# Cross-attention and mixture of experts on one core: another lead-in, tiles in smaller block groups, the output weight turned later, four output buffers

## Chip, core and metric

One core of one Trainium2 chip runs the whole program. The metric is the device time of one execution in microseconds. The inputs are float32.

## What is computed

```python
# x: (2, 2048, 512)   ctx: (2, 128, 512)   mask: (2, 1, 1, 128)
def attention(query, ctx, mask, W_out):            # 16 heads of 32
    energy = einsum('nqhd,nkhd->nhqk', q, k)       # q: layernorm(x), k = v = ctx
    energy = where(mask == 0, -1e20, energy)
    attn = softmax(energy / sqrt(512), axis=-1)
    return einsum('nhqk,nkhd->nqhd', attn, v).reshape(N, Q, 512) @ W_out.T

def ffn(x, proj_w, anchors, temp, w1, w2):         # 6 experts, hidden 256, top 2
    q = tanh(einsum('btd,ed->bte', x, proj_w) / 0.3)
    logits = -(6.0 - einsum('btd,ed->bte', q, anchors)) * 0.5 / clip(temp, 0.1)
    topk_logits, topk_idx = top_k(logits, 2)       # weights: their softmax
    h = gelu(einsum('btd,edh->bteh', x, w1))
    return einsum('bteh,ehd,bte->btd', h, w2, expert_weights)

x = x + attention(layernorm(x), ctx, mask, W_out)
x = x + ffn(layernorm(x), ...)
```

## The kernel before

All engines' programs are written out by hand in one fixed order; nothing is scheduled by a tool. Semaphores tie them together (`wait_ge`, `then_inc`). The 4096 rows are 32 row tiles of 128 (in the last part called token tiles, numbered `c`), four of them are a block, and there are eight blocks (`nblk`), the first four (`NB1`) of batch 0.

**Attention part.** It is a software pipeline over steps `s` from -3 to 44. In step `s` each engine does one piece for several row tiles or units at once; a unit is one block and one group of four heads (`unit(v)`), and there are 32. The lags are constants: a row tile is loaded at `L_LOAD = -3`, its statistics are taken on VectorE at `L_STAT = -1` (with four small GpSimd operations that make its scale), it is normalised on ScalarE (`xn`, L976) at `L_XN = 0`, turned by TensorE (L1667) and copied to `qT` (L938) at `L_XT = 1`. At `L_TOK = 5` TensorE forms a unit's scores by token (L1539) in four PSUM banks (4 to 7), one for each head, only to get their maxima, which VectorE takes (`nmax`, L1103) in the head order 3, 2, 0, 1. At `L_MT = 9` the maxima of a block are turned (L1687) into `mT`. At `L_KEY = 10` come the scores by key (L1560, L1563) in banks 0 to 3, and ScalarE's exponentials (`prob`, L930). At `L_PV = 11` come the row sums (L1697, bank 7) and the products with the values (L1722, bank 6); ScalarE makes the reciprocal of the sums from a logarithm and an exponential (`rden`, L956, L958), and VectorE makes `newton` (L1370) in the same step and `raw` (L1339) one step later. Both have to be done before TensorE may write the next unit's scores by token, because banks 6 and 7 are among the four. From `L_MID = 17` on each step also projects one row tile with the output weight (L1586 to L1588, three products of high and low parts), adds the residual (L1210), and makes the router's logits, choices and places.

**Setup.** Before step -3 the masked keys are turned and filled; the filled keys (`kfT`) are used by the scores by token, the selector rows (`selT`) by the scores by key. The output weight `woraw` is turned in four pieces (L1509), in steps 2 to 5 (`WT0 = 2`), into banks 2 and 3; ScalarE copies a piece to `woH` (L860), VectorE subtracts it for `woL` (L1093). Its first reader is step 17.

**Tables.** The rows of each expert are scattered to a region of their own in `xs_d` (L739). The expert part works on 69 tiles of 128 such rows. Which rows tile w has and which expert it is, stands in a table that VectorE computes. The first `T1 = 27` tiles are full tiles of the first four blocks; their list is made by `full_tiles()` and `first_list()` in steps 40 and 41. The other 42 come in classes: class c has the tiles that become complete, or begun, with the first NB1 + c blocks. Their list is made in slots 19 to 23 of the expert part. `TILES_OF` tells for a block how many tiles must be done before all its rows are.

**Expert part.** It is a loop of 76 slots; in slot j tile w = j - 2 is turned (L1763), w = j - 3 goes through the first layer (L1777 to L1779), w = j - 4 is turned again (L1787), w = j - 5 goes through the second (L1803 to L1805), and its result is copied to `ysb` (VectorE for w below 26, then ScalarE, L1032) and stored to `y_d` in slot w + 6 (SyncE, L641). `ysb` has two buffers, each used again when its store has landed. From slot 46 on a finished token tile is put together in each slot: two slots before, GpSimd gathers its two expert rows from `y_d` (L809, two indirect transfers); VectorE adds them, weighted, to the residual (`put_together`, L1408, L1410); SyncE stores it two slots later (L601) and loads a residual for 16 tiles later three slots after that (L607). Token tiles 28 to 31 need all 69 tiles and come after the loop. SyncE's queue is in order: xg loads, y stores, output stores and residual loads wait for each other.

## Time and profile before

| | us |
|---|---|
| median of three runs | 640.44 (638.33 to 643.96) |
| the profiled execution's own time | 639.05 |
| its span in the trace | 636.2 |
| TensorE matmuls busy | 557.3 (88%) |
| VectorE busy | 419.2 (66%) |
| ScalarE busy | 343.7 (54%) |
| GpSimd busy | 303.4 (48%) |

Busy time is the sum over a span whose parts have different limits, so a share says little by itself; a stretch and the wait that ends last in it say more. Times in the rows are from the start of the span.

### The profile page before, as it was taken

The page shows a single profiled execution, that of the slowest core. Times are in us where ns is not written, and L with a number is a line of the kernel's source. Part 1 is how long each engine was busy: PE and PEld are TensorE (multiplying, and loading weights), DVE is VectorE, ACT ScalarE, POOL GpSimd, SP SyncE. Part 2 cuts the span into 40 slices and gives each one's busy share as a digit, 9 for nine tenths or more (in the row PEclk, how much of TensorE's full clock was granted, in tenths as well). Part 3 has the DMA queues.
Part 4 walks back from the last instruction along what each step waited for, and adds up shares of the span by engine and source line. Part 5 has one row for each costly group of instructions (what it writes and reads, how often), then busy time and mean ns, then how long its engine had stood idle before and what let it go on. Part 6 is the DMA issues. An engine that isn't in the chain of part 4 may idle for free.

```text
span 636.2 us, 14210 instructions
## 1 busy us (share of the span) xinstructions
PE 557.3 (88%) x4472; PEld 409.1 (64%) x4472; DVE 419.2 (66%) x895; ACT 343.7 (54%) x664; POOL 303.4 (48%) x434
## 2 busy tenths in 40 slices
PE   5668899999999999899787999998999999999950
PEld 3554355565555555545475897887999998987730
DVE  4677777667678776748799555567843356666643
ACT  3648875777767656466556663532355544443420
POOL 5434765655548666485688041331000155555443
PEclk9779999999999999999997999998999999999995
DMA  5321132233213329373558374786567799999986
GB/s 167 101 67 51 52 97 88 83 101 100 100 50 101 134 84 344 104 265 133 171 177 282 103 246 157 242 281 216 191 224 233 220 293 357 401 405 405 365 298 186
DMA packets 60274, 122.07 MB, mean 192 GB/s; under 512 B 7718, under 2 KB 10790, under 8 KB 60204
## 3 DMA queue, kind: packets, MB, share of 16 engines
q1 hardware_dynamic: 49964, 87.61, 40.9%
q0 software_dynamic: 10240, 33.56, 14.8%
q8 instruction: 40, 0.66, 0.4%
q14 instruction: 30, 0.25, 0.1%
HBM read 67.93 MB, written 53.22 MB: 190 GB/s over the span
## 4 chain that ended last, share of the span: by engine, by line
PE 64%; DVE 13%; issue 10%; DMA 4%; ACT 4%; POOL 3%; SPq 0%; POOLq 0%; DVEq 0%; ACTq 0%
PE ps L1777 5%; PE ps L1779 4%; PE ps L1697 4%; PE ps L1778 4%; PE ps L1803 4%; PE ps L1805 4%; PE ps L1804 4%; PE ps L1763 4%; PE ps L1560 4%; PE ps L1539 4%; PE ps L1586 4%; PE ps L1588 3%; PE ps L1587 3%; PE ps L1722 3%; DMA y_d<-ysb 2%
## 5 line engine op out<-in xcount | busy, mean ns | idle before, releaser
L809 POOL DMA_INDIRECT yg<-y_d,y_row x64 | 66.7, 1041 | 129.0 <-DMA y_d<-ysb 74.6
L739 POOL DMA_INDIRECT xs_d<-x,to_row x64 | 66.8, 1043 | 70.0 <-DVE to_row L1185 34.2
L930 ACT ACTIVATE prob<-ps 128x512 f32<-128x512 f32 x128 | 65.9, 600 | 53.0 <-PE ps L1563 52.8
L1103 DVE TENSOR_REDUCE nmax<-ps 128x4 f32<-128x512 f32 x128 | 79.5, 685 | 21.4 <-PE ps L1539 21.4
L1777 PE MATMUL ps<-w1H,xgH 128*128 x276 | 84.0, 305 | 4.9 <-issue 4.4
L1421 DVE TENSOR_TENSOR xgL<-ps,xgH 128x512 fp32r<-128x512 f32 x69 | 47.5, 689 | 53.5 <-ACT xgH L1012 44.0
L1779 PE MATMUL ps<-w1L,xgH 128*128 x276 | 78.1, 283 | 0.0
L1778 PE MATMUL ps<-w1H,xgL 128*128 x276 | 77.9, 282 | 0.0
L1803 PE MATMUL ps<-w2H,hH 128*128 x138 | 60.3, 437 | 1.3 <-DVE ysb L1436 1.2
L769 POOL TENSOR_TENSOR atT<-less,raw 128x512 f32<-128x512 f32 x32 | 40.9, 1279 | 42.6 <-issue 36.8
L1777 PEld LDWEIGHTS ps<-w1H,xgH 128*128 128x128 f32 x276 | 52.8, 191 | 7.9 <-issue 7.6
L1032 ACT ACTIVATE ysb<-ps 128x512 f32<-128x512 f32 x43 | 25.8, 599 | 55.8 <-DMA y_d<-ysb 30.8
L1012 ACT ACTIVATE xgH<-ps 128x512 fp32r<-128x512 f32 x69 | 41.1, 595 | 25.3 <-PE ps L1763 21.7
L1805 PE MATMUL ps<-w2L,hH 128*128 x138 | 54.5, 395 | 0.0
L1586 PE MATMUL ps<-woH,atH 128*128 128x512 f32 x128 | 52.9, 413 | 1.5 <-DVE x L1210 1.2
L1804 PE MATMUL ps<-w2H,hL 128*128 x138 | 54.1, 392 | 0.0
L1778 PEld LDWEIGHTS ps<-w1H,xgL 128*128 128x128 f32 x276 | 53.0, 192 | 0.0
L1019 ACT ACTIVATE gel<-ps 128x256 f32<-128x256 f32 x69 | 26.6, 386 | 48.1 <-PE ps L1779 40.7
L1779 PEld LDWEIGHTS ps<-w1L,xgH 128*128 128x128 f32 x276 | 52.6, 191 | 0.0
L1429 DVE TENSOR_TENSOR hL<-ps,hH 128x256 fp32r<-128x256 f32 x69 | 29.1, 421 | 33.7 <-ACT hH L1025 29.4
L1539 PEld LDWEIGHTS ps<-kfT,qT 32*128 32x128 f32 x1024 | 33.5, 190 | 26.7 <-issue 26.3
L1588 PE MATMUL ps<-woH,atL 128*128 128x512 f32 x128 | 50.0, 391 | 0.0
(214 smaller groups left out, 1296.5 us busy)
## 6 DMA issues: line engine op xcount, KB each, us to landing
xg<-xs_d SPq DMA_DIRECT2D x69, 256.0 KB
y_d<-ysb SPq DMA_DIRECT2D x69, 256.0 KB
xin<-in_x SPq DMA_DIRECT2D x32, 256.0 KB, 2.7
x<-in_x SPq DMA_DIRECT2D x32, 256.0 KB, 3.0
x_d<-x SPq DMA_DIRECT2D x32, 256.0 KB
x2t<-x_d SPq DMA_DIRECT2D x32, 256.0 KB
out_x<-x2t SPq DMA_DIRECT2D x32, 256.0 KB
w1L<-in_L_ffn_w SPq DMA_DIRECT2D x6, 512.0 KB, 8.2
```

What stands on the lines that cost most here:

```text
L739: nc.gpsimd.indirect_dma_start(xs_d, bass.IndirectOffsetOnAxis(ap=to_row[:, n, k, t:t + 1], axis=0), x2[:, n % 4, t, :], None).then_inc(sc ...
L809: nc.gpsimd.indirect_dma_start(yg[:, c % RY, z, :], None, y_d[0:TILES_OF[c // 4] * P, :], bass.IndirectOffsetOnAxis(ap=y_row[:, c, z:z + 1 ...
L930: nc.scalar.activation(prob[v % 2][:, h, :], ps[:, B_SC + h, :], ACT.Exp, scale=scale).then_inc(exp_done, 1)
L1103: nc.vector.tensor_reduce(nmax[:, n % 2, :, g * hpg + h], ps[:, token_bank(h), :].rearrange("p (t k) -> p t k", t=4), axis=AX.X, op=ALU.ma ...
L1586: mm(o, h[:, g, :], woH[:, g, :], start=(g == 0), stop=False)
L1588: last = mm(o, l[:, g, :], woH[:, g, :], start=False, stop=(g == kchunks - 1))
L1777: mm(o, xgH[:, p, c, :], w1h[:, cols], start=(c == 0), stop=False)
L1778: mm(o, xgL[:, p, c, :], w1h[:, cols], start=False, stop=False)
L1779: last = mm(o, xgH[:, p, c, :], w1l[:, cols], start=False, stop=(c == kchunks - 1))
L1803: mm(o, hH[:, p, c, :], w2h[:, cols], start=(c == 0), stop=False)
L1804: mm(o, hL[:, p, c, :], w2h[:, cols], start=False, stop=False)
L1805: last = mm(o, hH[:, p, c, :], w2l[:, cols], start=False, stop=(c == halves - 1))
```

## The change

Four things are joined.

1. Lead-in. Statistics of the first four row tiles, the filled keys and the selectors are interleaved otherwise; the scores by token of units 1 and 3 go to banks 0 to 3 (`token_bank`, up to unit `SOON = 5`) and those of units 0, 2 and 4 to banks 4 to 7; the turned row tile goes to a bank that is free (`turned_bank`). `raw` of units 0 to 5 is formed in the same step as `newton`, before it.
2. Output weight. It is turned in steps 10 to 13 (`WT0 = L_KEY`), through one bank. ScalarE copies each piece twice, to `wot` and to `woH`; GpSimd forms `woL` from these. The router's projection follows in step 14. Small GpSimd constants move from steps 1 to 3 to steps 4 to 6.
3. Block groups. The full tiles of the first four blocks are listed with those of the first three blocks ahead. All tokens of the first three blocks are then complete after 32 tiles instead of 37. The last block is counted in two halves, so that token tiles 28 and 29 need 65 tiles and only 30 and 31 need all 69. Token tiles are put together from slot 41 on, five in six slots (slots 41 to 45, 47 to 51, ..., 68), those of the last two blocks in slots 70 to 75, and only 30 and 31 after the loop.
4. `ysb` has four buffers (`RW = 4`).

```diff
-    TILES_OF = [most_tiles(max(n + 1, NB1)) for n in range(nblk)]
-    CLASSES = nblk - NB1 + 1
+    TILES_OF = [T1 + EXPERTS - 1 if n + 1 < NB1 else most_tiles(n + 1) for n in range(nblk) for t in range(4)]
+    TILES_OF[4 * nblk - 4] = TILES_OF[4 * nblk - 3] = most_tiles(nblk - 0.5)
+    CLASSES = nblk - NB1 + 3
-    RY, RX, RD = 6, 16, 4
+    RY, RX, RD, RW = 6, 16, 4, 4
-        B_CNT, B_SEL, B_WT, B_FILL, B_KT = 2, 2, 2, 4, 6
+        B_CNT, B_SEL, B_WT, B_FILL, B_KT = 2, 2, 1, 4, 6
+        SOON = 5
-        def token_bank(h):
-            return B_MX + h
+        def token_bank(v, h):
+            return (B_MX if v >= SOON or v % 2 == 0 else B_SC) + h
+        def turned_bank(w):
+            v = w + L_XT - L_TOK
+            return B_XT if v <= 0 or v + 1 >= SOON else token_bank(v - 1, TOKEN_ORDER[0])
...
         def put_slot(c):
-            s = TILES_OF[0] + 9 + c
-            return s if s < SLOTS and TILES_OF[c // 4] < tiles else None
+            w = TILES_OF[0] + 9 + c + c // 5
+            if c // 4 >= nblk - 2:
+                w = TILES_OF[c] + 9 + c - TILES_OF.index(TILES_OF[c])
+            return w if w < SLOTS and TILES_OF[c] < tiles else None
-        WT0 = 2
+        WT0 = L_KEY
...
# GpSimd
+                c = s - WT0
+                if 0 <= c < kchunks:
+                    pool.wait_ge(s_woR, c + 1)
+                    pool.wait_ge(s_woH, c + 1)
+                    nc.gpsimd.tensor_tensor(woL[:, c, :], wot[:, c, :], woH[:, c, :], ALU.subtract).then_inc(s_woL, 1)
...
# ScalarE
-                    nc.scalar.activation(woH[:, c, :], ps[:, B_WT + c % 2, :], ACT.Copy).then_inc(s_woH, 1)
+                    nc.scalar.activation(wot[:, c, :], ps[:, B_WT, :], ACT.Copy).then_inc(s_woR, 1)
+                    nc.scalar.activation(woH[:, c, :], ps[:, B_WT, :], ACT.Copy).then_inc(s_woH, 1)
...
+                if 0 < s < 4:
+                    rows_normalised(s - L_XN)
+
                 w = s - L_XT
...
                     nc.scalar.activation(qT[n % 3][:, :, t * P:(t + 1) * P],
-                                         ps[:, B_XT, :].rearrange("p (k t) -> p k t", k=kchunks), ACT.Copy).then_inc(qT_done, 1)
+                                         ps[:, turned_bank(w), :].rearrange("p (k t) -> p k t", k=kchunks), ACT.Copy).then_inc(qT_done, 1)
+                setup(s)
...
+                if not 0 < s < 4:
+                    rows_normalised(s - L_XN)
+                if s == 3:
+                    filled_keys()
+                if s == L_TOK:
+                    selectors()
...
-                        after(act, y_out[p], 16 * n)
-                        nc.scalar.activation(ysb[:, p, :], ps[:, y_bank(w, p), :], ACT.Copy).then_inc(ya_done, 1)
+                        _, r, n = tl(i, k, L_DN, RW)
+                        after(act, y_out[r], 16 * n)
+                        nc.scalar.activation(ysb[:, r, :], ps[:, y_bank(w, p), :], ACT.Copy).then_inc(ya_done, 1)
...
# VectorE
             def attention(s):
-                d = s - L_DIV
...
+                if s >= L_MID + 1:
+                    raw_product(s - L_DIV)
...
+                setup(s)
+                if s <= L_MID - 1:
+                    raw_product(s - L_PV)
...
# TensorE, scores by token and by key
-                pe.wait_ge(qT_done, 4 * n + 4)
+                pe.wait_ge(qT_done, max(4 * n + 4, min(v + L_TOK - L_XT, 4 + SOON - 1)))
+                if v == 1:
+                    pe.wait_ge(s_selT, batches)
-                after(pe, mx_done, hpg * v)
+                after(pe, mx_done, hpg * (v if v >= SOON else v - 1))
...
+                after(pe, s_woH, min(v + L_KEY - WT0, kchunks))
```

On TensorE, from the key fill to the second scores by token, before (`xn` is the normalised row tile, `selk` the selector rows, `kfill` the filled keys):

```order
L1483 MATMUL ps<-kmask,pickb 128x512 x2
L1488 MATMUL ps<-ident,selk 128x128 x8
L1495 MATMUL ps<-ident,kfill 128x128 x8
L1667 MATMUL ps<-ident,xn 128x128 x8
L1509 MATMUL ps<-ident,woraw 128x128 x4
L1667 MATMUL ps<-ident,xn 128x128 x4
L1509 MATMUL ps<-ident,woraw 128x128 x4
L1667 MATMUL ps<-ident,xn 128x128 x4
L1509 MATMUL ps<-ident,woraw 128x128 x4
L1539 MATMUL ps<-kfT,qT_78 128x128 x16
```

and now:

```order
L1553 MATMUL ps<-kmask,pickb 128x512 x2
L1745 MATMUL ps<-ident,xn 128x128 x12
L1566 MATMUL ps<-ident,kfill 128x128 x8
L1745 MATMUL ps<-ident,xn 128x128 x4
L1559 MATMUL ps<-ident,selk 128x128 x8
L1606 MATMUL ps<-kfT,qT_78 128x128 x16
```

The row tiles are turned ahead of the filled keys and the selectors, and the output weight is gone from here.

On VectorE, the end of `first_list()` in step 41, before (`ntil` counts tiles of an expert, `whole` the full ones, `taken` and `some` belong to the two groups of the new list):

```order
L1261 TENSOR_REDUCE lexpert<-prod 128x1
L1262 TENSOR_SCALAR lst<-lexpert 128x1
L1271 TENSOR_SCALAR ntil<-first 128x6
L1272 TENSOR_SCALAR ntil<-ntil 128x6
L1273 TENSOR_TENSOR ntil<-ntil,whole 128x6
L1339 TENSOR_TENSOR raw<-ps,rden 128x512
```

and now:

```order
L1323 TENSOR_REDUCE lexpert<-prod 128x1
L1324 TENSOR_SCALAR lst<-lexpert 128x1
L1335 TENSOR_SCALAR taken<-first 128x12
L1336 TENSOR_SCALAR taken<-taken 128x12
L1337 TENSOR_TENSOR taken<-taken,some 128x12
L1338 TENSOR_TENSOR ntil<-taken 128x6
L1339 TENSOR_TENSOR ntil<-ntil,soon 128x6
L1407 TENSOR_TENSOR raw<-ps,rden 128x512
```

Two operations are added here, two more at the list's beginning, and `full_tiles()` a step earlier has fourteen instead of six.

On VectorE, in the expert slots about the fifth and sixth token tile, before (`x2t` is the residual that becomes the output, `yg` the gathered rows):

```order
L1408 SCALAR_TENSOR_TENSOR x2t<-yg,share,x2t 128x512 [waits yg_in4,x2t_in0]
L1410 SCALAR_TENSOR_TENSOR x2t<-yg,share,x2t 128x512 [waits half_done]
L1421 TENSOR_TENSOR xgL<-ps,xgH 128x512 [waits xh_done]
L1429 TENSOR_TENSOR hL<-ps,hH 128x256 [waits hh_done]
L1408 SCALAR_TENSOR_TENSOR x2t<-yg,share,x2t 128x512 [waits yg_in5,x2t_in1]
```

and now:

```order
L1477 SCALAR_TENSOR_TENSOR x2t<-yg,share,x2t 128x512 [waits yg_in4,x2t_in0]
L1479 SCALAR_TENSOR_TENSOR x2t<-yg,share,x2t 128x512 [waits half_done]
L1490 TENSOR_TENSOR xgL<-ps,xgH 128x512 [waits xh_done]
L1498 TENSOR_TENSOR hL<-ps,hH 128x256 [waits hh_done]
L1490 TENSOR_TENSOR xgL<-ps,xgH 128x512 [waits xh_done]
L1498 TENSOR_TENSOR hL<-ps,hH 128x256 [waits hh_done]
L1477 SCALAR_TENSOR_TENSOR x2t<-yg,share,x2t 128x512 [waits yg_in5,x2t_in1]
```

After five token tiles a slot without one is left.

## Rows read from the trace of the kernel before

**Rows 1.** Timeline, 0 to 30 us: start, us, engine, line, operation, [idle before].
```profile
7.76 3.17 PE L1483 MATMUL ps<-kmask,pickb 128*128 128x512 f32 x4
...
10.14 0.25 POOL L782 TENSOR_SCALAR nmr<-mrs 128x1 f32<-128x1 f32 x1
...
14.21 0.83 ACT L976 ACTIVATE xn<-xin,nmr,rstd 128x512 f32<-128x512 f32 x1
...
24.03 1.17 PE L1539 MATMUL ps<-kfT,qT 32*128 32x128 f32 x32
```

**Rows 2.** Timeline, 29 to 60 us: token scores, first scores by key.
```profile
31.76 1.17 PE L1539 MATMUL ps<-kfT,qT 32*128 32x128 f32 x32 [1.77 <-DVE nmax L1103]
32.13 0.69 DVE L1346 BATCH_NORM_STATS2 st<-xin 128x6 f32<-128x512 f32 x1
...
32.99 2.48 DVE L1103 TENSOR_REDUCE nmax<-ps 128x4 f32<-128x512 f32 x4
...
35.63 1.17 PE L1539 MATMUL ps<-kfT,qT 32*128 32x128 f32 x32 [2.10 <-DVE nmax L1103]
...
42.93 2.09 PE L1560 MATMUL ps<-qT,kT 32*128 32x512 f32 x8 [0.78 <-ACT mT L950]
```

**Rows 3.** Timeline, 55 to 63 us: one round of the ring.
```profile
55.86 1.17 PE L1539 MATMUL ps<-kfT,qT 32*128 32x128 f32 x32 [0.62 <-DVE raw L1339]
...
57.88 1.06 PE L1697 MATMUL ps<-prob,ones 128*32 128x512 f32 x8 [0.27 <-issue]
...
60.91 0.68 DVE L1339 TENSOR_TENSOR raw<-ps,rden 128x512 f32<-128x512 f32 x1
...
61.74 1.17 PE L1539 MATMUL ps<-kfT,qT 32*128 32x128 f32 x32 [0.62 <-DVE raw L1339]
```

**Rows 4.** Timeline of VectorE, 296 to 318 us.
```profile
303.55 0.69 DVE L1210 TENSOR_TENSOR x<-ps,x 128x512 f32<-128x512 f32 x1 [1.28 <-PE ps L1588]
...
310.50 0.17 DVE L1273 TENSOR_TENSOR ntil<-ntil,whole 128x6 f32<-128x6 f32 x1
...
312.06 1.13 DVE L1192 TENSOR_TENSOR wgt<-wsel,winv 128x24 f32<-128x24 f32 x1
```

**Rows 5.** Stretches: busy PE, PEld, DVE, ACT, POOL (count), clock, DMA share, GB/s.
```profile
500.00:550.00 50.00, 48.73 (x337) 43.92 (x336) 28.50 (x47) 23.94 (x55) 25.85 (x24) 1.00 0.92 317
...
550.00:560.00 10.00, 10.00 (x72) 9.13 (x71) 8.02 (x13) 4.25 (x11) 5.84 (x6) 1.00 1.04 405
...
590.00:600.00 10.00, 9.01 (x61) 7.69 (x60) 6.70 (x12) 3.56 (x10) 4.54 (x5) 1.00 1.04 394
```

**Rows 6.** The page: DMA queue, one group of ScalarE, one DMA issue.
```profile
q0 software_dynamic: 10240, 33.56, 14.8%
...
L1032 ACT ACTIVATE ysb<-ps 128x512 f32<-128x512 f32 x43 | 25.8, 599 | 55.8 <-DMA y_d<-ysb 30.8
...
xg<-xs_d SPq DMA_DIRECT2D x69, 256.0 KB
```

**Rows 7.** Timeline of TensorE: turns of xg tiles 55, 56 and 66.
```profile
557.88 0.60 PE L1763 MATMUL ps<-ident,xg 128*128 128x128 f32 x4
...
561.35 0.60 PE L1763 MATMUL ps<-ident,xg 128*128 128x128 f32 x4
...
601.85 0.60 PE L1763 MATMUL ps<-ident,xg 128*128 128x128 f32 x4
```

**Rows 8.** Timeline, 608 us to the end.
```profile
610.19 1.43 POOL L809 DMA_INDIRECT yg<-y_d,y_row  x1 [0.31 <-issue]
...
612.53 0.39 PE L1805 MATMUL ps<-w2L,hH 128*128 x1
...
614.47 0.60 ACT L1032 ACTIVATE ysb<-ps 128x512 f32<-128x512 f32 x1 [2.69 <-DMA y_d<-ysb]
...
617.91 0.95 POOL L809 DMA_INDIRECT yg<-y_d,y_row  x1 [6.30 <-DVE x2t L1410]
...
627.16 0.95 POOL L809 DMA_INDIRECT yg<-y_d,y_row  x1 [0.30 <-issue]
```

More of the change, by code:

```diff
@@ L257, in xattn_moe @@
         lst = sb("lst", [P, 2])
-        zero_row1 = sb("zero_row1", [P, EXPERTS])
-        bound = sb("bound", [P, EXPERTS, CLASSES + 1])
-        moveby = sb("moveby", [P, EXPERTS, CLASSES + 1])
-        change = sb("change", [P, EXPERTS * (CLASSES + 1)])
-        within = sb("within", [P, 2 * 4, EXPERTS * (CLASSES + 1)])
+        zero_row1 = sb("zero_row1", [P, 2, EXPERTS])
+        soon = sb("soon", [P, EXPERTS])
+        some = sb("some", [P, 2, EXPERTS])
+        taken = sb("taken", [P, 2, EXPERTS])
+        nsoon = sb("nsoon", [P, 1])
+        bound = sb("bound", [P, EXPERTS, PLACES])
+        moveby = sb("moveby", [P, EXPERTS, PLACES])
+        change = sb("change", [P, EXPERTS * PLACES])
+        within = sb("within", [P, 2 * 4, EXPERTS * PLACES])
         moved = sb("moved", [P, 2 * 4])
@@ L914, in exponentials, with rows_normalised @@
                     nc.scalar.activation(lexp[:], ldif[:], ACT.Exp).then_inc(lexp_done, 1)
+            def rows_normalised(w):
+                if live(w, ntile):
+                    n, t = w // 4, w % 4
+                    act.wait_ge(rstd_done, 4 * w + 4)
+                    act.wait_ge(x_in[t], 16 * (n + 1))
+                    after(act, xt1_ready, w - 1)
+                    nc.scalar.activation(xn[:, w % 2, :], xin[:, t, :], ACT.Identity, bias=nmr1[:, t, :],
+                                         scale=rstd1[:, t, :]).then_inc(xn_done, 1)
             def attention(s):
@@ L1051, in link, with statistics @@
                 dve.wait_ge(s_set, chain[0])
+            def statistics(w):
+                n, t = w // 4, w % 4
+                dve.wait_ge(x_in[t], 16 * (n + 1))
+                after(dve, mv_done, w - 3)
+                nc.vector.bn_stats(st1[:, t, :], xin[:, t, :]).then_inc(st_done, 1)
+                dve.wait_ge(st_done, w + 1)
+                after(dve, rstd_done, 4 * (w - 3))
+                nc.vector.bn_aggr(mv1[:, t, :], st1[:, t, :]).then_inc(mv_done, 1)
             link(nc.vector.tensor_scalar(m01[:], maski[:], 0.0, None, ALU.not_equal))
@@ L1637, in prefix @@
                                   allones[:].bitcast(F32R), sel[:, t:t + 1, :].bitcast(F32R).to_broadcast([P, 4 - t, EXPERTS]), start=False, stop=(t == 3))
+                    if n == nblk - 1:
+                        for t in range(2):
+                            last = mm(ps[:, b, PL0 + 5 * EXPERTS:PL0 + 6 * EXPERTS], allones[:].bitcast(F32R),
+                                      sel[:, t, :].bitcast(F32R), start=(t == 0), stop=(t == 1))
                     last.then_inc(pl_ready, 1)
```

200 lines of the change are left out of this document (109 added, 91 removed).

## The prediction

> **What bounds the kernel now.** I read the span stretch by stretch, since the limit changes. The reader should see five things.
>
> First, the start. The four row tiles of block 0 must be normalised, turned and copied before any scores can be made. VectorE, ScalarE and TensorE hand each other one tile at a time. The scale of the first tile is there at 10.14 + 0.25 = 10.39 us, TensorE has finished the key fill at 7.76 + 3.17 = 10.93 us, and yet ScalarE writes the first normalised tile only at 14.21 and the first scores by token start at 24.03 [rows 1]. In between stand the two key copies, the two selector copies and the output weight.
>
> Second, from 24 to 43 us each step takes 35.63 - 31.76 = 3.87 us [rows 2]: scores 1.17, then four maxima 2.48 on VectorE, and TensorE waits for these because the four banks are the same ones. The first scores by key come at 42.93.
>
> Third, up to step 17 a ring through three engines sets the pace [rows 3]: scores at 55.86, one maximum, row sums at 57.88, their logarithm and its exponential on ScalarE, newton and then raw (60.91) on VectorE, next scores at 61.74. The period is 5.88 us. From step 18 TensorE is nearly full until about 300 us, then VectorE carries the chain to about 350 us; the first tile table stands in that chain [rows 4].
>
> Fourth, in the expert part TensorE needs 561.35 - 557.88 = 3.47 us for a slot, but the ten slots to 601.85 take 40.50 us [rows 7]: 5.8 us too many. What is late is a buffer. ScalarE stood 30.8 us in waits for stores of y_d before its copies into ysb [rows 6]. The stores are late because the DMA engines are full: 405 GB/s at a share of 1.04, 394 near the end, while the mean of 500 to 550 us was 317 [rows 5].
>
> Fifth, the end. TensorE is done at 612.53 + 0.39 = 612.92 us and the span ends at 636.2. The last copy waited 2.69 us for a buffer, the last store had landed by 617.91, and only then do eight gathers of four token tiles start, the last at 627.16 [rows 8].
>
> **Start, steps -1 to 9.** Statistics of tiles 0 and 1 move ahead of the selector rows, so the scale comes about 0.6 us earlier, at 9.8. TensorE now turns tile 0 right after the key fill, at 10.95. Each round is a normalisation (0.83, [rows 1]), a turn of four transposes (0.60, [rows 7]; up to twice that while TensorE has the lower of its clocks) and a copy (0.60 for this size, [rows 8]), and the normalisation of the next tile stands ahead of the copy: 1.3 to 1.8 us a round. VectorE gives the fourth statistic only after the filled keys. I make three rounds end near 16.2, then the fill transposes, the fourth turn and the selector transposes (eight, four and eight: 2.3 us if all follow at once): first scores at 18.5, 5.5 us earlier. In steps 5 to 9 the scores alternate between banks 4 to 7 and 0 to 3. The step is then VectorE's: 2.48 + 0.87 (from the statistics at 32.13 to the maxima at 32.99, [rows 2]) + 0.1 = 3.45, so 0.4 less for each of three steps. One step is late by about 1 us, because the selector copies now stand on ScalarE before the second scores. The last hand-over (maxima, nmhl, turn, mT) loses a half microsecond of TensorE queue. I put the first scores by key at 36.2 instead of 42.93: **6.7 us earlier**. Bounds: 3 (TensorE slow at the start, one more late load) and 9.
>
> **Output weight, steps 10 to 14.** It leaves a stretch in which ScalarE waits for the others and goes to one in which it stands in the ring. Each of four steps gets four more transposes (0.60), and two ScalarE copies (0.6 each, one of them new) that stand ahead of the logarithm of the ring. The sums end about 0.4 us later, and the logarithm starts 0.5 later. In step 10 there is no sum yet, but the next scores by key wait for woH: 1.1 us. Sum 1.1 + 3 x 0.45 + 0.1 for projT = **2.5 us later**. If all of it hides it is 0; if nothing does, 4 x (0.6 + 1.2) = 7.2. I stay near the lower end: between the maximum and the sums' logarithm the ring leaves ScalarE some two microseconds, and only what the copies need beyond that counts. The subtraction for woL goes from VectorE to GpSimd, which is off the ring except in step 13. Putting raw before newton changes nothing in the ring, as both must be done before the next scores. Net for both parts: **-4.2 us**, from 0 to -9.
>
> **Tile tables.** The first table gets eight more VectorE operations of about 0.2 us (0.17 is a typical one, [rows 4]) at 300 us and four more in the list at 307. The eight run into an idle of 1.28 us that VectorE spends waiting for the projection at 303.55 [rows 4], so 1.65 - 1.28 = 0.4 us shows. The four are in the chain: 0.8. Sum **+1.2**; 0.8 if all eight hide. The later tables gain two classes, one operation and two small matmuls beside expert slots, where VectorE is busy 28.50 of 50 us [rows 5]: at nothing, 0.5 us if not.
> Two operations of the same size took 1.13 us at 312.06 [rows 4] and 0.17 elsewhere, with GpSimd at work beside the long ones. The Trainium skill, SBUF — State Buffer, section "Who interferes with whom", says that a VectorE operation with two SBUF inputs and a GpSimd operation that reads SBUF shut each other out for a whole instruction. By that rule this group could cost about 4 us rather than 1.2.
> From the rows alone the upper bound is 12 x 0.35, a third of the operations being long: 4.3.
>
> **Gathers in 5 of 6 slots, 5 slots earlier, and four y buffers.** A slot loads one xg tile and stores one y tile (0.26 MB each, [rows 6]). A token tile costs 0.26 MB four times: two gathers (33.56 MB in 128 indirect transfers), one residual load, one store. Before, with a token tile in each slot, 0.524 + 1.049 = 1.573 MB in 3.47 us asks 454 GB/s; the rows show 405 [rows 5], so it falls behind. After, with 5 of 6 slots, 1.398 MB ask 403 GB/s, at the capacity and no more, and the five earlier slots use a time when 317 was moved. Four ysb buffers let a store be late by about 10 us. So I take the whole 5.8 us back: **-5.8**. Bounds: 0 if the stores stay late past four buffers, and -7 if slots before tile 56 had lost a little too.
>
> **The end.** The last half block waits for all 69 tiles, the half before it for 65, so four gathers move ahead of the last store. Relative to before: GpSimd ends tile 27's gathers at 610.19 + 1.43 = 611.6, then six steps of 1.3 us (9.25 us for seven gaps at the end, [rows 8]) bring the first gather of tile 31 to about 619.7 and its second to 621.0. The last store follows the matmuls by one copy, 613.7 with no buffer wait. From the end of that copy to the first gather went 617.91 - 615.07 = 2.8, so it is there by 616.5 and does not bind. 621.0 instead of 627.16: **-6.1**. The landing, the combination and the last store, 9.0 us from 627.16 to the end, stay as they are. Bounds: -4 (the store lands late and binds) and -8 (less traffic, quicker landings).
>
> **Sum.** -4.2 + 1.2 - 5.8 - 6.1 = -14.9. The profiled execution was 639.05 us, span 636.2 and 2.85 around it: 639.05 - 14.9 = 624.2. The median of the three runs lies 1.4 above it, so I say **624.5**.
>
> **Rivals.**
> (a) The DMA engines stay full and the stores stay late, so the slots gain nothing; the end still has four gathers less (5.3). -4.2 + 1.2 - 5.3 = -8.3: 631. For it: 403 is no margin, and the window rows are means over 10 us. Against: four buffers.
> (b) The lead-in gives nothing, since the output weight eats it: -10.7: 628.5. For it: ScalarE stands in the ring in those steps. Against: 6.7 before 2.5.
> (c) The transfers carry less than the rows show when gathers, residual loads and y traffic all mix for 28 slots. Those slots took 28 x 3.47 + 5.8 = 103.0 us. Halfway between 405 and 317, at 361 GB/s, they would take 28 x 1.398 / 0.361 = 108.4 us: +5.4 - 8.3 = -2.9, 636. The rows show 405 for 30 us on end [rows 5], which speaks against it.
> The Trainium skill, DMA: Bandwidth & Descriptors, section "Where 436 GB/s comes from", says that between HBM and SBUF a side of about 358 GB/s binds; by that rule (c) holds, at 109.3 us and 637, and the trace disagrees with 405 GB/s.
> (d) Slower: the same mechanism, deeper. SyncE's queue is in order; if a combination waits for its gather, the store of its rows blocks the xg loads behind it, and each slot then lasts as long as its transfers. The time passes the old one by 1% once 28 x 1.398 / c is over 103.0 + 8.3 + 6.4 = 117.7 us, that is below c = 333 GB/s. At the 317 of 500 to 550 us it is 123.5: +20.5 - 8.3 = +12.2, 653. For it: that mean holds at a share of 0.92. Against: the windows after it show 405, so 317 was demand and not capacity.
>
> **Chances.** Forecast 0.62 (its own range 617 to 629), (a) 0.12, (b) 0.12, (c) 0.09, (d) 0.05. The range reaches from 616 to 635. Over 1% (6.4 us, about what a measurement can tell from no change) faster means below 634: forecast, (a) and (b), 0.86. Within 1%: (c) and a part of the rest, 0.09. Slower: 0.05.
>
> **What would show it.** The first scores by token near 18.5 us, the first by key near 36, four steps after them at 6.3 to 6.5 us, and step 18 some 4 us earlier. First list 0.8 us longer. No waits of ScalarE for y_d stores worth naming, xg turns 3.47 us apart through tile 66, DMA near 400 GB/s from the fifth slot of gathers on but stores landed in time. After the last matmul some 17 us instead of 23.3, with four gathers after the last store. Wrong it would be if gathers or stores from slot 41 on hold back the xg loads, or if steps 10 to 13 run over 7 us.

## The result, and the profile after

The changed kernel takes **622.82 us** (median of four runs, 619.53 to 623.75) against 639.73 for the kernel before (median of four, 638.33 to 643.96). The ratio is 0.9717, 95% interval 0.9664 to 0.977. The forecast was 624.5, with a range from 616 to 635. The profiled execution took 619.53 us, span 617.7, against 639.05 and 636.2: 18.5 us less span, where the sum of the prediction had 14.9.

The stretches of the span, each read from TensorE's starts (turns of `xg` are counted from tile 0; by this count the turns at 557.88, 561.35 and 601.85 of [rows 7] are tiles 57, 58 and 68, not 55, 56 and 66):

| | before | after | difference | predicted |
|---|---|---|---|---|
| first scores by token | 24.03 | 17.22 | -6.8 | -5.5 |
| scores by token of step 10 | 45.20 | 36.20 | -9.0 | -6.7 |
| ... of step 18 | 94.33 | 87.56 | -6.8 | -4.2 |
| ... of step 36 | 258.05 | 251.82 | -6.2 | -4.2 |
| turn of tile 2 | 350.86 | 346.05 | -4.8 | -3.0 |
| end of the last matmul | 612.92 | 597.28 | -15.6 | -8.8 |
| end of the span | 636.2 | 617.7 | -18.5 | -14.9 |

The timeline of TensorE and VectorE in the start, of the changed kernel (start, us, engine, line, operation, idle before); it answers to [rows 1, 2]:

```profile
7.79 2.97 PE L1553 MATMUL ps<-kmask,pickb 128*128 128x512 f32 x4
...
10.62 0.66 PE L1745 MATMUL ps<-ident,xn 128*128 128x128 f32 x4
...
17.22 1.17 PE L1606 MATMUL ps<-kfT,qT 32*128 32x128 f32 x32
...
21.38 1.17 PE L1606 MATMUL ps<-kfT,qT 32*128 32x128 f32 x32 [2.41 <-issue]
...
23.83 1.17 PE L1606 MATMUL ps<-kfT,qT 32*128 32x128 f32 x32 [0.69 <-ACT qT L981]
...
25.83 2.45 DVE L1151 TENSOR_REDUCE nmax<-ps 128x4 f32<-128x512 f32 x4
...
26.27 1.17 PE L1606 MATMUL ps<-kfT,qT 32*128 32x128 f32 x32 [0.69 <-ACT qT L981]
...
29.02 2.45 DVE L1151 TENSOR_REDUCE nmax<-ps 128x4 f32<-128x512 f32 x4
...
33.94 2.09 PE L1632 MATMUL ps<-qT,kT 32*128 32x512 f32 x8 [0.78 <-ACT mT L994]
```

TensorE now makes the scores of a unit while VectorE still reads the unit before. So three of its steps are 2.44 us, each with a wait of 0.69 us for ScalarE's copy of the turned row tile, and no longer VectorE's: the maxima start 3.19 us apart (25.83, 29.02). The first step is 4.16 us (17.22 to 21.38): the selector copies end on ScalarE at 21.28, just ahead of the second scores. TensorE waits for VectorE only once, at the end of the steps:

```profile
31.02 0.63 PE L1745 MATMUL ps<-ident,xn 128*128 128x128 f32 x4 [1.12 <-DVE nmax L1151]
```

The ring with the output weight in it, the same timeline, 49 to 54 us; it answers to [rows 3]:

```profile
49.85 1.06 PE L1782 MATMUL ps<-prob,ones 128*32 128x512 f32 x8
...
50.02 0.59 ACT L890 ACTIVATE wot<-ps 128x512 f32<-128x512 f32 x1
50.49 0.60 ACT L891 ACTIVATE woH<-ps 128x512 fp32r<-128x512 f32 x1
...
50.98 0.60 ACT L1000 ACTIVATE rden<-ps 128x512 f32<-128x512 f32 x1
...
52.34 0.69 DVE L1407 TENSOR_TENSOR raw<-ps,rden 128x512 f32<-128x512 f32 x1 [0.64 <-ACT rden L1002]
...
52.95 0.68 DVE L1440 TENSOR_TENSOR newton<-ps,rden 128x512 f32<-128x512 f32 x1
...
53.97 1.17 PE L1606 MATMUL ps<-kfT,qT 32*128 32x128 f32 x32 [0.89 <-DVE newton L1440]
```

The logarithm (L1000) follows the second copy without a gap, and the next scores by token follow the second of the two products. The steps from 12 to 17 last 6.25, 6.59, 6.25, 6.14 and 5.98 us, against 5.88 before (6.26 in the second of them).

Stretches of the expert part of the changed kernel (busy time and count of PE, PEld, DVE, ACT, POOL; then clock, DMA share, GB/s); they answer to [rows 5]:

```profile
500.00:550.00 50.00, 50.00 (x348) 45.25 (x347) 33.42 (x55) 25.33 (x59) 23.84 (x23) 1.00 1.04 392
...
550.00:560.00 10.00, 10.00 (x71) 9.04 (x70) 5.97 (x10) 5.03 (x12) 6.03 (x6) 1.00 1.04 407
...
590.00:600.00 10.00, 7.27 (x39) 5.67 (x37) 5.54 (x9) 3.59 (x8) 7.87 (x7) 1.00 0.92 293
```

The DMA engines are as full as at their fullest before (1.04, 392 and 407 GB/s), and for longer; yet TensorE is busy all the time. Its turns (answering to [rows 7]) are:

```profile
553.02 0.60 PE L1847 MATMUL ps<-ident,xg 128*128 128x128 f32 x4
...
556.48 0.60 PE L1847 MATMUL ps<-ident,xg 128*128 128x128 f32 x4
...
587.49 0.60 PE L1847 MATMUL ps<-ident,xg 128*128 128x128 f32 x4
```

Ten slots, 553.02 to 587.49, take 34.47 us where they took 40.50. In the list of waits ScalarE's copy into `ysb`, 30.8 us for stores before [rows 6], does not wait for a store at all.

The end of the changed kernel, answering to [rows 8]:

```profile
596.88 0.40 PE L1889 MATMUL ps<-w2L,hH 128*128 x1
...
597.31 0.60 ACT L1074 ACTIVATE ysb<-ps 128x512 f32<-128x512 f32 x1 [0.94 <-issue]
...
598.70 0.41 SPq L662 DMA_DIRECT2D y_d<-ysb  x1
...
600.39 0.95 POOL L836 DMA_INDIRECT yg<-y_d,y_row  x1 [0.30 <-issue]
...
604.62 0.99 POOL L836 DMA_INDIRECT yg<-y_d,y_row  x1 [3.28 <-DMA y_d<-ysb]
...
608.93 0.95 POOL L836 DMA_INDIRECT yg<-y_d,y_row  x1 [0.30 <-issue]
```

Four gathers follow the last store instead of eight, but the first of the four waits for that store: 6.7 us from the end of the copy (597.91) to 604.62, where it was 2.8 before, there behind a copy that had itself waited 2.69 us for a store [rows 8]. From the last matmul to the end of the span it is 20.4 us instead of 23.3.

### The profile page after: what moved, and what is told of

The parts are those of the page before. It is cut to its first block, busy times and chain, and to the rows that moved or that the text cites. A ratio compares the mean times of both kernels' runs of the same rounds, so it can differ in the third digit from the quotient of the medians.

```text
span 617.7 us, 14277 instructions
## 1 busy us (share of the span) xinstructions
PE 545.1 (88%) x4474; PEld 402.4 (65%) x4474; DVE 424.3 (69%) x905; ACT 345.5 (56%) x668; POOL 308.8 (50%) x438
## 3 DMA queue, kind: packets, MB, share of 16 engines
q0 software_dynamic: 10240, 33.56, 14.9%
## 4 chain that ended last, share of the span: by engine, by line
PE 64%; DVE 16%; issue 8%; ACT 6%; POOL 2%; DMA 2%; POOLq 0%; SPq 0%; DVEq 0%; ACTq 0%
PE ps L1861 5%; PE ps L1863 5%; PE ps L1862 5%; PE ps L1887 5%; PE ps L1889 5%; PE ps L1888 5%; PE ps L1847 5%; PE ps L1632 4%; PE ps L1658 4%; PE ps L1782 4%; PE ps L1660 3%; PE ps L1659 3%; ACT prob L970 3%; PE ps L1807 3%; PE ps L1606 2%
## 5 line engine op out<-in xcount | busy, mean ns | idle before, releaser
L1863 PE MATMUL ps<-w1L,xgH 128*128 x276 | 76.8, 278 | 0.0
L1659 PE MATMUL ps<-woL,atH 128*128 128x512 f32 x128 | 50.0, 391 | 0.0
```

Of the source, the lines that this page charges most:

```text
L1659: mm(o, h[:, g, :], woL[:, g, :], start=False, stop=False)
L1863: last = mm(o, xgH[:, p, c, :], w1l[:, cols], start=False, stop=(c == kchunks - 1))
```

## The experiments

Each ratio is to the kernel before, measured beside the variant (medians of 638.43 to 639.87), with its 95% interval. The totals of one kernel differ by some microseconds from execution to execution, so the readings rest on two stretches of one profile each: **slots**, from the turn of tile 23 to the end of the last matmul, and **tail**, from there to the end of the span. Eight profiles (changed, and the last seven rows) have the same expert slots, but for the last tiles in two of them. Their slots took 165.3 to 167.8 us, so a difference of up to 2.5 us says little. The tails with four gathers behind the last store lie between 18.6 and 21.2 us.

| kernel | median, us | ratio (interval) | slots | tail |
|---|---|---|---|---|
| before | 639.73 | 1 | 174.5 | 23.3 |
| changed | 622.82 | 0.9717 (0.9664 to 0.977) | 165.3 | 20.4 |
| before, four `ysb` | 636.77 | 0.9963 (0.9934 to 0.9991) | 173.6 | 23.2 |
| changed, two `ysb` | 627.36 | 0.9831 (0.9776 to 0.9887) | 171.0 | 19.0 |
| every slot | 632.62 | 0.9897 (0.9857 to 0.9938) | 173.8 | 19.0 |
| every slot to 19 | 627.23 | 0.9792 (0.9766 to 0.9819) | 170.3 | 18.7 |
| from slot 46 | 629.35 | 0.9821 (0.9772 to 0.9871) | 171.6 | 21.2 |
| last block whole | 625.85 | 0.982 (0.9783 to 0.9856) | 166.0 | 23.7 |
| old banks | 624.98 | 0.9799 (0.9758 to 0.9839) | 165.3 | 19.5 |
| weight not turned | 619.7 | 0.9721 (0.9691 to 0.9751) | 166.4 | 18.6 |
| one copy | 622.26 | 0.9758 (0.9726 to 0.979) | 165.3 | 19.5 |
| newton first | 625.36 | 0.9762 (0.9735 to 0.9789) | 167.8 | 20.7 |
| ScalarE's stores | 625.42 | 0.978 (0.9749 to 0.9812) | 166.4 | 19.8 |
| filled | 621.31 | 0.9702 (0.9661 to 0.9743) | 166.0 | 19.2 |

### Buffers or rate

Four buffers alone, in the kernel before:

```diff
-        ysb = sb("ysb", [P, 2, emb])
+        ysb = sb("ysb", [P, RW, emb])
...
-                        after(act, y_out[p], 16 * n)
+                        after(act, y_out[r], 16 * n)
```

> The kernel before with four ysb buffers and nothing else changed. Theory 'buffers' (what was late was the buffer, and two more of them, 2 x 3.47 = 6.9 us of lateness, hide nearly all of it): no waits of ScalarE on stores of y_d but a few at the very end, last matmul 6 to 8 us earlier than 612.92, 632 to 634 us in all. Rival 'rate' (each slot asks 1.57 MB in 3.47 us, 454 GB/s against 405, a deficit of about 0.4 us in each of 28 slots; the backlog then shows at the xg loads and the gathers instead): last matmul at most 3 us earlier, 637 to 640 us.

Slots 173.6 against 174.5, last matmul 2.1 us earlier, total 0.4% less (636.77 us, just under the rival's 637): the rival "rate" was right. In the profile ScalarE's wait for stores is gone, and these waits (us in total, times, longest) stand in its place:

```profile
POOL yg L809 <- DMA y_d<-ysb: 10.3, 2, 6.0
...
PEld ps L1765 <- DMA xg<-xs_d: 5.1, 6, 1.4
...
PE ps L1765 <- DMA xg<-xs_d: 2.2, 3, 1.0
```

The stretches from 540 to 600 us show 405, 405 and 402 GB/s at a share of 1.04: the same full engines. A buffer more only hands the lateness on, from the stores to the loads.

Two buffers in the changed kernel:

```diff
-    RY, RX, RD, RW = 6, 16, 4, 4
+    RY, RX, RD, RW = 6, 16, 4, 2
```

> The changed kernel with two ysb buffers again. Theory 'buffers': the stores are late by more than one slot at a DMA share of 1.04, so ScalarE waits again and the last matmul moves from 597.28 to 600.5 or later; 626 us or more. Rival 'rate' (five token tiles in six slots keep the transfers within capacity, the buffers are spare): waits on y_d stores under 3 us in sum, last matmul within 1 us of 597.28, 622 to 624 us.

Slots 171.0, 5.7 us more than with four; here "buffers" was right. The waits of this kernel:

```profile
ACT ysb L1074 <- DMA y_d<-ysb: 21.3, 13, 4.7
```

One of them alone was 4.70 us, ahead of the copy at 522.98, and TensorE's two slots around it took 10.97 us instead of 6.9. So with the old slots two more buffers are worth 0.9 us, which is not clear of the scatter, with the new ones 5.7; the slots (with their block groups) are worth 3.5 us with two buffers and 8.3 with four. Neither half explains the gain; each needs the other.

Token tiles in every slot from 41:

```diff
-            w = TILES_OF[0] + 9 + c + c // 5
+            w = TILES_OF[0] + 9 + c
```

> The changed kernel with a token tile in every slot from slot 41 to 64 (no slot left out), four buffers. Theory 'buffers': the 24 slots ask 454 GB/s, fall behind by up to 24 x 0.4 = 10 us, which is more than four buffers hold; a stall of 2 to 4 us late in that stretch, given back by nothing; end as now or 1 us shorter since slots 65 to 69 carry no gathers: 623 to 626 us. Rival 'rate' (the left-out slot is what keeps the pace): 627 us or more. If it costs nothing (within 1 us of 622.8), the left-out slots are worth nothing by themselves.

Slots 173.8: 8.5 us more, the expectation of "rate". But the profile shows a second cause. At 563.20 GpSimd had waited for the store of the last expert tile that token tile 20 needs:

```profile
563.20 0.95 POOL L836 DMA_INDIRECT yg<-y_d,y_row  x1 [7.27 <-DMA y_d<-ysb]
...
570.44 0.75 DVE L1477 SCALAR_TENSOR_TENSOR x2t<-yg,share,x2t 128x512 f32<-128x512 f32 x1 [5.41 <-DMA yg<-y_d,y_row]
...
572.71 0.19 PEld L1861 LDWEIGHTS ps<-w1H,xgH 128*128 128x128 f32 x1 [3.58 <-issue]
```

GpSimd waits for the store, VectorE in its combination for the gather, and behind that stand the subtractions TensorE needs. A second kernel took this away, and left the rate up to tile 19:

```diff
-            w = TILES_OF[0] + 9 + c + c // 5
+            w = TILES_OF[0] + 9 + c + (4 if c >= 20 else 0)
```

> The changed kernel with token tiles 0 to 19 in every slot from 41 to 60 and 20 to 23 where the changed kernel has them (65 to 68). With every slot to tile 23 the run was slower by 9 to 10 us, and in it GpSimd waited 7.27 us for a store of y_d ahead of the gathers of tile 20, since these come only one slot behind the store of the last expert tile that tile 20 needs. Theory 'caught up with its block': that wait alone made the loss; here it is gone and the pace holds: from the turn at slot 25 to the last matmul about 165 to 168 us as in the changed kernel, 622 to 625 us. Rival 'rate': 454 GB/s asked in 20 slots against 405 leaves a backlog of 20 x 0.4 = 8 us that four buffers do not hold: that stretch takes 170 us or more, 628 us or more.

Slots 170.3, the edge of what "rate" asked, and 627.23 us, just short of its 628. So 5.0 of the 8.5 us come with a token tile in each of the first twenty slots, and the other 3.5 with token tiles 20 to 23 in slots 61 to 64. These 3.5 hold the wait for the block, but also four more slots at the full rate, since slots 61 to 64 have no token tile in the second kernel; the two were not separated.

The old slots (one each from 46 to 69) with four buffers and the new groups:

```diff
-            w = TILES_OF[0] + 9 + c + c // 5
+            w = TILES_OF[0] + 14 + c
```

> The changed kernel with the old slots for the first 24 token tiles (one in every slot from slot 46 to 69), four buffers, the last eight as changed. Theory 'buffers': a backlog without time to clear before the end, last matmul 2 to 4 us later than 597.28 and the end longer by 1 us: 625 to 628 us. Rival 'rate': the last matmul 5 us or more later, 628 us or more. If it is within 1 us of 622.8, start and rate of the token tiles are worth nothing once there are four buffers.

Slots 171.6, 6.3 more; 629.35 us, and the last matmul at 608.06 (part of that lateness stems from the start, which ran at a lower clock). That is "rate" again. The loads of `xg` are late by 6.1 us in sum, and with a token tile in every slot from 46 to 75 there is none in which the backlog clears.

### The end

The last block not counted in halves:

```diff
-    TILES_OF[4 * nblk - 4] = TILES_OF[4 * nblk - 3] = most_tiles(nblk - 0.5)
```

> The changed kernel, but token tiles 28 and 29 wait for all 69 tiles again, so that eight gathers follow the last store. Theory 'four gathers less' (they cost 1.3 us each on GpSimd after the landing): the last gather starts 5.3 us later than 608.93, if the last store lands at the same 604.6; 627 to 629 us. Rival 'the last store is late because of them' (the gathers of 28 and 29, issued at 596.2 to 600.4, stand before the last store's packets in full DMA engines): without them the store lands near 600.7, the first of eight gathers starts then, the last at about 609.6, and the whole is within 1.5 us of 622.8.

The tail is 23.7, against 20.4 and, in the other profiles with the changed tail, 18.6 to 21.2: the half block is worth 2.5 to 5 us, 3.3 by the changed kernel's own profile. The first gather came at 602.44, 5.0 us after the end of the last copy (596.82 + 0.60), with no gathers of tiles 28 and 29 ahead. So these explain at most 1.7 of the 6.7 us, and even that is not shown: in the ten other profiles with the changed tail, with those gathers ahead, this time is 4.9 to 7.3 us. The last of the eight gathers started at 611.33, 2.4 later than 608.93, not 5.3 and not 0.7.

Why the store lands later than the 2.8 us of the kernel before can be read from the kernel before with four `ysb`:

```profile
610.86 0.60 ACT L1033 ACTIVATE ysb<-ps 128x512 f32<-128x512 f32 x1 [1.19 <-PE ps L1807]
...
615.53 0.94 POOL L809 DMA_INDIRECT yg<-y_d,y_row  x1 [6.01 <-DMA y_d<-ysb]
```

It has the old tail, but its last copy need not wait for a buffer, and then the gather starts 4.1 us after the copy. Counted from the last matmul it is 4.7 us (610.82 to 615.53), and 5.0 in the kernel before (612.92 to 617.91). The lateness moved from the copy to the store.

The last four stores issued by ScalarE:

```diff
+        OWN = 4
...
+                        if w >= tiles - OWN:
+                            act.wait_ge(ya_done, w + 1 - BY_ACT)
+                            nc.scalar.dma_start(y_d[w * P:(w + 1) * P, :], ysb[:, r, :]).then_inc(y_out[r], 16)
```

> The changed kernel, but the stores of the last four expert tiles are issued by ScalarE itself right behind its copy, and not by SyncE. Theory 'queue': the last store is late (gathers of tiles 30 and 31 start 6.7 us after the end of the last copy, against 2.8 before) because it stands behind output stores and waits in SyncE's order; from a queue of its own the gathers start 4 to 4.5 us after the copy, and the last store of the program comes 2 to 2.5 us earlier: 620.5 us, time from the last matmul to the end about 17.5 us. Rival 'engines full': the store's packets share the sixteen DMA engines with gathers, and another queue changes nothing: gathers start 6 to 7 us after the copy, 622.8 us, tail 19 to 20.5.

The gathers began at 609.24, 4.9 us after the copy's end. That is near what "queue" expects, but four profiles in which SyncE issues the stores have 4.9 to 5.1 us as well (two `ysb`, weight not turned, every slot to 19, newton first), so the queue's part is not shown. And the copy itself came late, and nothing was gained (tail 19.8):

```profile
603.75 0.60 ACT L1075 ACTIVATE ysb<-ps 128x512 f32<-128x512 f32 x1 [2.27 <-remote]
```

The profile does not name what it waited for. In the program the copy waits for two things, its matmuls and the store that used its buffer four tiles earlier, and the matmuls had ended at 601.63. So by elimination, which no row shows, it waited for that store. The same row with 2.33 us stands in the profile of newton first, where SyncE issues all stores, 2.75 us behind the last matmul. Four buffers are then not always enough at the very end; why in these two profiles and not in the others stays open.

### The start and the ring

Scores by token in banks 4 to 7 throughout:

```diff
-        SOON = 5
+        SOON = 0
```

> The changed kernel with all scores by token in banks 4 to 7 again, as before. Theory: the other order alone gives the 6.8 us up to the first scores by token (17.22), the banks only the 2.2 us between these and the first scores by key; so first scores by token at 17.2, then steps of 3.87 us, first scores by key at 36.1 instead of 33.94, 624 to 625.5 us. Rival: the ring afterwards is bound by its own period and absorbs it, 622.8 within 0.7, with step 18 where it was (87.56). Other rival: the turn of the row tiles waits too, 627 us or more.

The steps are 3.86 and 3.87 us again (23.13, 26.99, 30.86), against 2.44: this the banks do. How much of it lasts the run does not settle, since its clock was lower in the same stretch (0.83 in 10 to 20 us and 0.56 in 30 to 40, against 1.00 and 0.83 in the changed kernel's): first scores at 18.96 instead of the expected 17.2, first scores by key at 40.07 instead of 36.1. And its median of 624.98 lies 2.2 us above with overlapping intervals.

The output weight neither turned nor copied by ScalarE (the projection then uses it unturned):

```diff
-                    nc.scalar.activation(wot[:, c, :], ps[:, B_WT, :], ACT.Copy).then_inc(s_woR, 1)
-                    nc.scalar.activation(woH[:, c, :], ps[:, B_WT, :], ACT.Copy).then_inc(s_woH, 1)
...
+                    nc.gpsimd.tensor_copy(woH[:, c, :], woraw[:, c, :]).then_inc(s_woH, 1)
```

> The changed kernel, in which the output weight is not turned: TensorE's sixteen transposes and ScalarE's eight copies of steps 10 to 13 are left out, and GpSimd copies and subtracts the weight as it was loaded (so the projection uses it unturned, with the same instructions). Theory: these cost 2.3 to 2.7 us in the ring (the lead over before shrinks from 9.0 at step 10 to 6.7 at step 17): scores by token of step 18 at 85.0 instead of 87.56, 620.3 us. Rival: the lead shrinks for another reason (raw ahead of newton, or TensorE's queue), and step 18 stays within 0.7 us of 87.56.

From step 10 to step 18 it takes 49.80 us (36.20, 86.00) against 51.36: the weight costs 1.6 us, not 2.3 to 2.7. Step 18 came at 86.00, not at 85.0. Steps 14 to 17 are still 6.06, 6.21 and 5.98 us.

Newton ahead of raw:

```diff
-                if s <= L_MID - 1:
-                    raw_product(s - L_PV)
...
                 d = s - L_PV
...
                       .then_inc(newton_done, 1)
+                if s <= L_MID - 1:
+                    raw_product(s - L_PV)
```

> The changed kernel with newton ahead of raw again in steps 11 to 16, raw still in the same step. What is asked: without the turned weight, steps 14 to 17 still took 6.06, 6.21 and 5.98 us against 5.88 before. Theory 'order of the two': newton waits only for the reciprocal, raw also for the products; raw first and newton after it make the next scores start 1.54 us after raw's start (0.83 before), in part because the bank that newton reads is released last; putting newton first gives back 0.1 to 0.2 us a step: from step 11 to step 18 46.29 us becomes 45.2 to 45.7, the total is 0.6 to 1 us less. Rival: the two take as long in either order and the lengthening comes from the maxima or ScalarE; 46.3 within 0.3, no difference in the total.

From step 11 to step 18 45.58 us instead of 46.29, and the steps are 6.07, 6.48, 5.95, 6.03 and 5.87: the order of the two products costs 0.7 us. The total, 625.36 us, did not show it. In the profile two things stand against it: the start ran at a lower clock (below; step 18 at 89.72 instead of 87.56), and the slots, which the edit does not touch, took 2.5 us longer. Its rows at 20 to 50 us:

```profile
20.00:30.00 10.00, 6.91 (x104) 5.80 (x104) 8.59 (x17) 4.21 (x7) 4.58 (x22) 0.66 0.22 69
30.00:40.00 10.00, 8.53 (x84) 6.32 (x81) 6.53 (x12) 3.89 (x7) 4.34 (x14) 0.50 0.27 77
40.00:50.00 10.00, 8.15 (x108) 4.85 (x104) 6.69 (x12) 9.20 (x18) 3.90 (x7) 0.99 0.10 28
```

One copy fewer, VectorE subtracting straight from the bank:

```diff
-                    nc.scalar.activation(wot[:, c, :], ps[:, B_WT, :], ACT.Copy).then_inc(s_woR, 1)
...
+                    nc.vector.tensor_tensor(woL[:, c, :], ps[:, B_WT, :], woH[:, c, :], ALU.subtract).then_inc(s_woL, 1)
```

> The changed kernel with one ScalarE copy of each piece of the output weight instead of two; VectorE subtracts straight from the bank, in the place ahead of raw where it idles, and the next scores by key wait for that. Theory (a copy ahead of the logarithm costs its 0.47 us in each of three steps of the ring and 0.5 at the first): step 18 at 85.7 to 86.3 instead of 87.56, 621.2 us. Rival (the subtraction takes the place of the copy, since the scores by key start later by the same half microsecond): step 18 within 0.5 us of 87.56, 622.8 us.

From step 12 to step 17, at full clock in both, 31.31 us against 31.21, and no difference in the total (622.26 and 622.82): over these steps the rival was right. Step 18 itself, at 91.76, can't be compared with 87.56, since the start ran at a lower clock (0.66 in 20 to 30 us). In step 10 the next scores by key wait 2.22 us for the subtraction.

TensorE's idle filled, with newton first:

```diff
+                if s == L_TOK:
+                    for c in range(16):
+                        nc.tensor.transpose(ps[:, B_WT, (c % 4) * P:(c % 4 + 1) * P], ident[:], ident[:])
...
```

> The changed kernel with newton ahead of raw in steps 11 to 16, and with sixteen more transposes of the identity in step 5, behind the turned row tile, and four in step 9, behind the turned maxima, into bank 1, which nobody reads there: they fill 2.41 us and 0.78 us in which TensorE is idle. In three of the profiles with this lead-in (every slot to 19, slot 46, newton first) the granted clock was 0.63 to 0.66 in 20 to 30 us and 0.50 to 0.69 in 30 to 40, in three others 1.00 and 0.83, and the time from the first scores by token to step 18 was 72.2 to 73.0 us against 70.3. Theory 'the idle before the second scores by token lets the clock fall': with it filled the clock is 1.00 in 20 to 30 us in the profile, first scores to step 18 take 69.6 us (70.3 less 0.7 for newton), the times of single executions spread less, and the median is 620 to 621 us. Rival 'the fall comes from elsewhere': clock 0.6 to 0.7 there again, 72 us or more, median 624 to 626 us. Other rival: the transposes delay the second scores, step 6 later than 21.7 us, no gain.

The rows of the profile, in the place of those above:

```profile
20.00:30.00 10.00, 7.52 (x128) 6.24 (x127) 9.08 (x17) 5.27 (x9) 4.36 (x21) 1.00 0.35 91
30.00:40.00 10.00, 7.44 (x90) 5.63 (x91) 7.16 (x15) 4.83 (x9) 4.41 (x14) 0.75 0.25 71
40.00:50.00 10.00, 8.03 (x88) 4.68 (x86) 6.60 (x12) 8.21 (x17) 4.09 (x7) 0.91 0.10 28
```

The clock held at 1.00 in 20 to 30 us, and the steps there are 2.45 us. It fell elsewhere instead: the turns of the filled keys took 1.92 us ahead of the filling (1.04 in the changed kernel's profile), so the first scores came at 18.73 us, and step 10 was slow. First scores to step 18 took 70.8 us, neither the 69.6 of the theory nor the 72 of its rival. The median is 621.31, 4 us below newton first without filling, with intervals of the ratio that just overlap (0.9661 to 0.9743, 0.9735 to 0.9789). It is the lowest complete version here, 1.5 us below the changed kernel, but the intervals of these two overlap widely: better than the changed kernel is not shown.

## Why the prediction was right, and where its terms were off

**Start.** Forecast -6.7, measured -9.0 in the profiled execution. Two terms were mis-sized. One is "I make three rounds end near 16.2, then the fill transposes": the third turn ends at 14.26 + 0.63 = 14.89, and the fill transposes follow it at once, not behind the copy that ends the round at 15.65. So the first scores come at 17.22 instead of 18.5.

```profile
14.26 0.63 PE L1745 MATMUL ps<-ident,xn 128*128 128x128 f32 x4 [0.89 <-ACT qT L981]
```

The other is "The step is then VectorE's": 3.45. With the banks alternating TensorE runs ahead of VectorE with steps of 2.44 us; VectorE's are 3.19, and only the last hand-over brings them together. This gives the other 1.0 us, first scores by key at 33.94 instead of 36.2. A part of the 9.0 is neither: the kernel before did not have the full clock in its start either (granted 0.86, 0.80, 1.00 and 0.66 in the four stretches from 10 to 50 us, against 1.00, 1.00, 0.83 and 1.00). With four `ysb`, the same program up to there, it reached step 18 at 93.09 instead of 94.33, so against that profile the lead is 5.5 us and not 6.8. And in three of the profiles with the same start the clock fell, and the lead over 94.33 at step 18 was 4.5 us (from slot 46), 4.6 (newton first, with 0.7 of its own) and 3.9 (every slot to 19) instead of 6.8. The forecast of -4.2 for start and weight lies between these. By step 36 the lead of 6.8 was 6.2; the forecast had nothing for that stretch.

**Output weight.** Forecast +2.5, measured +2.2 (lead 9.0 at step 10, 6.8 at step 18). The runs split it otherwise than the prediction did: 1.6 for the weight, 0.7 for "putting raw before newton changes nothing in the ring". That step was wrong: with newton first each of the steps 11 to 16 is 0.1 to 0.3 us shorter. That newton needs only the reciprocal and the sums, and raw also the products, fits this.

**Tables.** Forecast +1.2, measured +1.4 (lead 6.2 at step 36, 4.8 at the turn of tile 2). The list is longer by 0.65 us (4.21 before, 4.86 after), forecast 0.8. The eight operations took 1.8 us where "0.4 shows"; two others behind them, in a place they moved, were long:

```profile
296.87 1.34 DVE L1235 TENSOR_TENSOR pslot<-pick,slot 128x48 f32<-128x48 f32 x1
...
298.48 0.94 DVE L1240 TENSOR_SCALAR to_row<-place 128x8 uint32<-128x8 f32 x1
```

They were 0.21 and 0.44 us before. Each now runs beside an operation of GpSimd and ends within 0.1 us of it:

```profile
296.87 1.28 POOL L796 TENSOR_TENSOR atT<-less,raw 128x512 f32<-128x512 f32 x1 [0.90 <-POOL less L792]
298.10 1.29 POOL L817 TENSOR_TENSOR atL<-atT,atH 128x512 fp32r<-128x512 f32 x1
```

The eight operations make raw later, and GpSimd's product, which waits for raw, now starts together with `pslot`. So they cost more than their own time: they brought two others beside GpSimd's work. In all eleven variants of the changed kernel the two take 1.33 or 1.34 and 0.94 us as well. The residual's addition started 4.2 us earlier than before instead of 5.8. 0.9 us of this was caught up by the newton that follows, which had waited 0.83 us before. The Trainium skill, SBUF — State Buffer, section "Who interferes with whom", would have a VectorE operation with two SBUF inputs wait whole instructions beside a GpSimd operation that reads SBUF. The trace agrees for `pslot`, and for the only two of the thirty-five operations of the two tables that took over 0.3 us: 0.43 and 0.63, each ending with a GpSimd instruction (at 302.09 and 302.76, against 302.07 and 302.73). The 4 us that the prediction gave for this case did not come, because GpSimd was idle for most of the second table (4.29 us up to 307.02); and beside its 128x4 operation of 1.06 us at 293.60 the trace disagrees, since the small ones with two inputs kept their 0.17 us.

**Slots.** Forecast -5.8. Measured -9.2 in the stretch from the turn of tile 23; another 1.5 lie between the turns of tiles 21 and 23 (12.24 against 10.72 us), which took 9.1 to 12.5 us in the other profiles of either kind and belong to no part of the change. The term left out what the kernel before lost ahead of and behind the ten slots: 1.6 us in one slot at 528.52 (5.11 instead of 3.47) and 1.3 behind the last turn (11.07 us to the last matmul, now 9.79). The mechanism was right as put: demand at capacity, with buffers that let a store be late; the runs with one of the two alone bear it out. Rival (a) was the case "rate right, buffers not enough"; the run with two buffers is that case, at +5.7.

**End.** Forecast -6.1, measured -2.9 (-2.0 to -4.7 in the other profiles). The step that failed: "From the end of that copy to the first gather went 617.91 - 615.07 = 2.8, so it is there by 616.5 and does not bind". The copy of that row had waited 2.69 us for a store. The prediction took this wait away and kept the 2.8 behind it: 3.6 us from the last matmul to the gather. Before it was 5.0, in the changed kernel it is 7.3 (6.7 behind the copy), and the store binds by 3.3 us.

**Rivals.** (b), (c) and (d) did not happen. (c) and (d) fell with the capacity: 410 GB/s in 560 to 570 us with gathers, residual loads and stores mixed. By the Trainium skill, DMA: Bandwidth & Descriptors, section "Where 436 GB/s comes from", about 358 would have bound; the trace of the changed kernel disagrees, with 406 to 410 GB/s in each ten microseconds from 530 to 580.

**Sum.** It came out too small by 3.6 us of span, and that is the balance of larger errors: 2.6 too little for start and weight, 5.0 for the slots with tiles 21 to 23, against 3.2 too much for the end and 0.8 for what lies between step 18 and tile 2. That they partly cancel is luck. The median came nearer still (622.8 against 624.5), because the profiled execution was the quickest of the four. The 624.5 leaves out a part of its own sum, too: 624.2 and the 1.4 by which the median lay above the profiled execution make 625.6.

## What to carry to other kernels

When a buffer is late because the transfer engines are full, ask for both: work per slot just within the capacity, and buffers for the lateness of a single transfer. Each alone gave 0.9 and 3.5 us here, both together 9.2. Cut the tail by what has to follow the last store, and count how late that store lands from the last matmul on: a landing time read behind a copy that had itself waited for a buffer is too short. Operations added to one engine also move those behind them; look at what they then run beside. Where two engines hand over through banks, a second set of banks lets the first run ahead, and its pace is no longer the second's, until something needs the second's result.

## What was unexpected of the hardware

The same instructions, with the same idle of TensorE, ran in the first 35 us at different clocks. In the changed kernel's profile and most others the granted clock was 1.00 (2.4 GHz) in 20 to 30 us; in those of slot 46, newton first, every slot to 19 and one copy it was 0.63, 0.66, 0.66 and 0.66, partly at the lower level, 1.2 GHz, at which the scores by token take 2.09 us instead of 1.17 (newton first has 0.50, the lower level alone, in 30 to 40 us). In newton first it fell at 23 us, after an idle of 2.41 us and the next scores; the changed kernel had the same 2.41 us and it did not fall. What decides it is open. From the first scores to step 18 it is worth 2.0 to 2.6 us (72.3 to 72.9 in slot 46 and every slot to 19 against 70.3, and 72.2 in newton first). The four runs of the changed kernel fit this: 619.53 at a mean clock of 0.981, and 622.76 to 623.75 at 0.972 to 0.975; the other three have no trace. The kernel before shows the same in its two profiles (0.66 and 0.84 in 40 to 50 us). A profile of a kernel with gaps in its start is one of several starts, and a term of a few microseconds has to be read at the same clock.
